# A two-part transformer block: a dense mixture of eight experts becomes a routed one of 40 sorted tiles

## The reference, cut

```python
x = L0_attn_x                                   # (2, 1024, 128): 2 rows, 2048 tokens
xn = _layernorm(x)
x = x + transformer(xn) + moe(xn)

def transformer(x):                             # L = 4 layers, H = 16 heads of 8, F = 512
    for i in range(4):
        x = x + mha(layer_norm(x, ln1), causal + alibi mask)
        xn = layer_norm(x, ln2)
        x = x + gelu(xn @ ffn1.T + b) @ ffn2.T + b
    return layer_norm(x, final)

def moe(xf):                                    # E = 8 experts, the best 2 of a token
    logits = xf @ router_w + router_b
    top_w, sel = top_k(logits, 2)
    gates = softmax(top_w)
    for i in range(8):
        out_i = gelu(xf @ w1[i] + b1[i]) @ w2[i] + b2[i]
        acc = acc + out_i * sum(gates * (sel == i))
    return acc
```

## Time and profile before

| | us |
|---|---|
| time, median of 3 runs | 1606.52 |
| lowest and highest of them | 1605.92, 1608.01 |
| the profiled execution | 1611.84 |
| its span | 1610.0 |
| TensorE busy | 1391.6 |
| VectorE busy | 1046.6 |
| ScalarE busy | 999.9 |
| GpSimd busy | 220.1 |

### The profile page before, as it was taken

The page is one execution under the profiler, slowest core; times in us unless marked ns, Lnnn a source line. Parts: engine busy times, 40 slices in busy tenths (PEclk is TensorE's granted clock), DMA queues, the critical chain, the costliest instruction groups (busy, mean ns, idle before and its releaser), DMA issues.

```text
span 1610.0 us, 36678 instructions
## 1 busy us (share of the span) xinstructions
PE 1391.6 (86%) x12960; PEld 710.0 (44%) x12960; DVE 1046.6 (65%) x2259; ACT 999.9 (62%) x1214; POOL 220.1 (14%) x399
## 2 busy tenths in 40 slices
PE   3789898899889998798988998799998989889974
PEld 2444344454435344353443544344444535444343
DVE  5657666776676765666677766567667766676625
ACT  2055776568666775557865686565866577656841
POOL 4001200121010300112001210013001120011001
PEclk9579999999999999899999999899999999999997
DMA  5111313103021311203120130301211031201010
GB/s 184 56 29 32 97 32 99 30 30 105 24 74 32 96 32 46 75 26 97 32 74 30 30 110 20 99 17 60 82 46 58 19 97 31 78 30 31 5 47 13
DMA packets 82666, 88.87 MB, mean 55 GB/s; under 512 B 8744, under 2 KB 76080, under 8 KB 82480
## 3 DMA queue, kind: packets, MB, share of 16 engines
q1 hardware_dynamic: 82480, 86.43, 17.7%
HBM read 54.15 MB, written 33.55 MB: 54 GB/s over the span
## 4 chain that ended last, share of the span: by engine, by line
PE 67%; DVE 14%; issue 7%; ACT 7%; DMA 2%; SPq 2%; DVEq 0%; POOL 0%; ACTq 0%
PE PS L775 16%; PE PS L740 13%; PE PS L700 12%; PE PS L691 10%; DVE mx L996 7%; PE PS L757 4%; PE PS L721 2%; PE PS L745 2%; ACT PR L586 2%; PE PS L763 2%; DMA x<-orec 1%; DVE hb L920 1%; ACT hb L568 1%; PE PS L725 1%; DVE st L889 1%
## 5 line engine op out<-in xcount | busy, mean ns | idle before, releaser
L996 DVE TENSOR_REDUCE mx<-PS 128x1 f32<-128x512 f32 (+3 forms) x1280 | 773.1, 633 | 354.9 <-PE PS L745 204.1
L586 ACT ACTIVATE PR<-PS 128x1024 f32<-128x1024 f32 (+3 forms) x768 | 610.7, 808 | 441.0 <-PE PS L763 248.1
L740 PE MATMUL PS<-Kop,Qop 64*128 64x512 bf16 (+3 forms) x1536 | 415.5, 341 | 105.0 <-DVE mx L996 93.1
L757 PE MATMUL PS<-Qop,Kop 64*128 64x512 bf16 (+3 forms) x1536 | 368.3, 335 | 19.3 <-ACT PR L586 17.7
L740 PEld LDWEIGHTS PS<-Kop,Qop 64*128 64x128 bf16 x1536 | 128.4, 94 | 557.7 <-DVE mx L996 419.0
L775 PE MATMUL PS<-PR,vbuf 128*32 128x512 f32 (+3 forms) x3072 | 335.0, 509 | 0.4 <-ACT PR L586 0.4
L700 PE MATMUL PS<-wE,hb 128*128 128x128 f32 x1536 | 204.9, 284 | 14.6 <-ACT mrow L558 4.7
L700 PEld LDWEIGHTS PS<-wE,hb 128*128 128x128 f32 x1536 | 182.1, 193 | 33.6 <-issue 14.4
L745 PE MATMUL PS<-idb,mk 64*128 64x64 bf16 x2048 | 196.0, 193 | 0.0
L745 PEld LDWEIGHTS PS<-idb,mk 64*128 64x128 bf16 x2048 | 166.7, 97 | 40.7 <-issue 5.9
L763 PE MATMUL PS<-idb,mk 64*128 64x64 bf16 x2048 | 180.4, 191 | 0.0
(11 more groups left out here) (76 smaller groups left out, 940.6 us busy)
## 6 DMA issues: line engine op xcount, KB each, us to landing
Qop<-qst SPq DMA_DIRECT2D x64, 256.0 KB, 2.9
Kop<-kst SPq DMA_DIRECT2D x64, 256.0 KB, 3.2
...
wE<-in_moe SPq DMA_DIRECT2D x8, 514.0 KB, 3.6
...
Qop<-mrow SPq DMA_DIRECT2D x256, 3.0 KB
```

Of the source, the lines that this page charges most:

```text
L586: act.activation(PR[:, c % 4, :, 0:n], PS[:, 2 * (c % 2):2 * (c % 2) + 2, 0:n], ACT.Exp)\
L740: last = pe.matmul(PS[:, 5 + k % 2, n * e:n * e + n], Qop[r, par, a, P * i:P * i + P], Kop[r, kb, a, 512 * c:512 * c + n], start=True, sto ...
L757: last = pe.matmul(PS[:, 2 * (c % 2) + j, 0:n], Kop[r, kb, a, P * kt:P * kt + P], Qop[r, par, a, q0:q0 + n], start=True, stop=not DIAG[t])
L996: dve.tensor_reduce(mx[:, par, i, 2 * heads[0] + j:2 * heads[-1] + j + 1:2, c], PS[:, 5 + k % 2, 0:n * len(heads)].rearrange("p (h n) -> p ...
```

## The change

The experts are computed for the tokens that chose them alone. In the prologue each of the 4096 pairs of a token and one of its two experts gets a slot: pairs are ranked within their expert by two products with a triangle and with ones, and by scans on VectorE (`routing`, four steps between the maxima of the first unit). Each expert's pairs fill whole tiles of 128; 40 tiles are enough for every distribution. GpSimd writes the normalised tokens to their slots in memory (`scatter`, 32 indirect DMAs in units 0 and 1 of phase 0), to `xs`, which a DMA has filled with zeros. Four tiles are a group, and there are ten groups. For a group SyncE reads the four experts' numbers into a register, loads four weight tiles `wG`, biases `bG` and tokens `xG` (`group_in`); TensorE transposes the tokens ("xt"), makes h and y tile by tile; SyncE writes y to `ys` (`group_out`). In phase 7 GpSimd reads each pair back (`gather`, 32 indirect DMAs in units 0 and 1) and adds both of a token, times their gates, to the input (`combine`, unit 2).

`CHUNKS` now has X0, X1 and two groups, E0 in unit 2 and E1 in unit 3. Phase 0 has one group (E1), odd phases two, even phases one (E1), phase 7 none. X0 and X1 have their GELUs in one slot, (1, 3). X's h goes out through ScalarE, E's through VectorE.

```diff
-CHUNKS = (("E", 0), ("X", 0), ("X", 1), ("E", 1), ("E", 2), ("E", 3))
-HBUF = (0, 1, 0, 1, 0, 1)
-GELUS = ((0, 10), (0, 22), (1, 7), (2, 10), (2, 17), (3, 10))
...
-ON_SCALAR = [(k, f) for k in (0, 3, 5) for f in range(FT)] + [(4, 2), (4, 3)]
+CHUNKS = (("X", 0), ("X", 1), ("E", 0), ("E", 1))
+HBUF = (0, 1, 0, 1)
+GELUS = ((1, 3), (1, 3), (2, 11), (3, 11))
+XT_AT = {2: (2, 3), 3: (3, 3)}
+H_AT = (((0, 18), (0, 19), (0, 20), (0, 21)), ((0, 23), (1, 0), (1, 1), (1, 3)),
+        ((2, 4), (2, 6), (2, 8), (2, 10)), ((3, 4), (3, 6), (3, 8), (3, 10)))
+Y_AT = (((1, 8), (1, 8), (1, 9), (1, 9)), ((1, 11), (1, 12), (1, 13), (1, 14)),
+        ((2, 14), (2, 15), (2, 16), (2, 17)), ((3, 14), (3, 15), (3, 16), (3, 17)))
...
+FIRST_PLAN, LAST_PLAN = plan((3,), False, True), plan((0, 1), True, False, turns=3)
+ODD_PLAN, EVEN_PLAN = plan((0, 1, 2, 3), True, True), plan((0, 1, 3), True, True)
...
+            def group_in(g):
+
+                for i in range(GROUP):
+                    e = sp.value_load(expert_of[0:1, ds(GROUP * g + i, 1)], min_val=0, max_val=E - 1)
+                    sp.dma_start(wG[:, i, :], moe[ds(e, 1), :, :].rearrange("l p n -> (l p) n")).then_inc(S["c_g"], 16)
+                    sp.dma_start(bG[:, i, :], rb_b2[ds(e + 1, 1), :].to_broadcast([P, D])).then_inc(S["c_g"], 16)
+                sp.dma_start(xG[:, :, :], xsv[ds(g, 1), :, :, :].rearrange("g p t d -> (g p) t d")).then_inc(S["c_g"], 16)
...
+            sp.wait_ge(S["c_const"], 16 * 13)
+            sp.dma_start(xs.rearrange("(t p) d -> p t d", p=P), zero[:, :].unsqueeze(1).to_broadcast([P, TILES, D]))\
+                .then_inc(S["c_zero"], 16)
             for b in range(B):
                 for dst, src in ((kfill, kcov), (qfill, qcov)):
...
+                            if half == 0 and j == 2 and f is not None and b == 1:
+                                group_out(group_of(2, b, f), base + number(contents, "y", 2) + 1)
+                                group_in(group_of(3, b, f))
+                            if half == 0 and j == 3:
+                                group_out(group_of(3, b, f), base + number(contents, "y", 3) + 1)
...
+            def scatter(first, last):
+
+                for k in range(first, last):
+                    pool.indirect_dma_start(out=xs[:, :], out_offset=bass.IndirectOffsetOnAxis(ap=slot[:, k:k + 1], axis=0),
+                                            in_=xe[:, k % NT, :], in_offset=None).then_inc(S["c_xs"], 16)
...
+                    if q is None and j < 2:
+                        gather(16 * j, 16 * j + 16)
+                    if q is None and j == 2:
+                        wait_apart(pool, S["c_both"], 16 * RANKS)
+                        for half in range(4):
+                            combine(half // 2, half % 2)
...
-                pe.matmul(PS[:, bank, :], w[:, P * f:P * f + P], src, start=True, stop=True).then_inc(S["s_full"], 1)
...
+                    for m in range(FT):
+                        last = pe.matmul(PS[:, bank, P * m:P * m + P], wG[:, f, P * m:P * m + P], xGT[:, P * f:P * f + P],
+                                         start=True, stop=True)
...
-                    for j in range(4):
-                        t = 4 * c + j
-                        last = dve.scalar_tensor_tensor(out=acc[:, t, :], in0=PS[:, bank, P * j:P * j + P],
-                                                        scalar=gate[:, t, ds(p, 1)], in1=acc[:, t, :],
-                                                        op0=ALU.mult, op1=ALU.add)
+                    last = dve.tensor_tensor(yG[:, :, :], PS[:, bank, :].rearrange("p (t d) -> p t d", t=4), bG[:, :, :], ALU.add)
```

More of the change, by code:

```diff
@@ L33 @@
 U32 = mybir.dt.uint32
+I32 = mybir.dt.int32
 ALU = mybir.AluOpType
@@ L172, in build @@
         rb = sb("rb", [P, E])
-        b2e = sb("b2e", [E, D])
+        tri = sb("tri", [P, P])
+        ones = sb("ones", [P, 2 * P])
+        zero = sb("zero", [P, P])
+        bound = sb("bound", [P, RANKS])
+        place = sb("place", [P, TILES])
         finw = sb("finw", [P, 2, D])
@@ L240, in build @@
         S = {n: sem(n) for n in names}
-        c_wE = [sem(f"c_wE{i}") for i in range(2)]
         c_ldl = [sem(f"c_ldl{i}") for i in range(2)]
@@ L476, in max_parts, with gather, combine @@
                                    ALU.subtract).then_inc(S["s_mpool"], 1)
+            def scatter(first, last):
+                for k in range(first, last):
+                    pool.indirect_dma_start(out=xs[:, :], out_offset=bass.IndirectOffsetOnAxis(ap=slot[:, k:k + 1], axis=0),
+                                            in_=xe[:, k % NT, :], in_offset=None).then_inc(S["c_xs"], 16)
+            def gather(first, last):
+                for k in range(first, last):
+                    pool.indirect_dma_start(out=both[:, k // NT, k % NT, :], out_offset=None, in_=ys[:, :],
+                                            in_offset=bass.IndirectOffsetOnAxis(ap=slot[:, k:k + 1], axis=0))\
+                        .then_inc(S["c_both"], 16)
+            def combine(row, c):
+                tiles = half_tiles(row, c)
+                n = 4 * (2 * row + c)
+                for k, g in enumerate((g1, g2)):
+                    pool.tensor_tensor(both[:, k, tiles, :], both[:, k, tiles, :],
+                                       g[:, tiles].unsqueeze(2).to_broadcast([P, 4, D]), ALU.mult).then_inc(S["s_both"], 1)
+                for k in range(2):
+                    wait_apart(pool, S["s_both"], n + 2 + k)
+                    pool.tensor_tensor(xin[:, tiles, :], xin[:, tiles, :], both[:, k, tiles, :], ALU.add)\
+                        .then_inc(S["s_both"], 1)
             def phase(p, b, f, q, base, contents):
@@ L610, in phase @@
                                     turn_out(base + n, U + 1, 1 - par, 0)
-                                if kind == "h" and which in ON_SCALAR:
+                                if kind == "xt":
+                                    xt_out(base + n)
+                                if kind == "h" and CHUNKS[which[0]][0] == "X":
                                     h_out(base + n, which[0], which[1], b)
@@ L782, in phase @@
                 row = 1 - b
-                place = f if b == 1 else q
-                g0 = 0 if f is None else gelus_before(p)
-                done = [k for k in range(6) if CHUNKS[k][0] == "E" or f is not None]
+                g0 = gelus_before(b, f)
+                done = chunks_of(b, f, q)
                 for j in range(PH):
@@ L957, in v_out, with out_of_bank @@
                                   ALU.add).then_inc(S["s_taken"], 1)
-            def out_of_bank(n, kind, which, p, biases, b, row, bank=7):
+            def out_of_bank(n, kind, which, g, biases, b, row, bank=7):
                 if kind == "h":
@@ L963, in out_of_bank @@
                 if kind == "y":
-                    y_out(n, which, p, biases, row, bank)
+                    y_out(n, which, g, biases, row, bank)
                 if kind == "wo":
@@ L1004, in maximum, with ln_step @@
                         .then_inc(S["s_negm"], 1)
-            def ln_step(idx, row, c, first, now, ready):
+            def ln_step(idx, row, c, first, now, ready, src=xr):
                 (j, k), (j0, s0) = now, first
@@ L1031, in phase @@
                             for n, (spots, kind, which) in enumerate(contents):
-                                if spots[-1] == now and not (kind == "h" and which in ON_SCALAR):
-                                    out_of_bank(base + n, kind, which, p, 4 * p, b, row)
+                                if spots[-1] == now and not (kind == "h" and CHUNKS[which[0]][0] == "X"):
+                                    out_of_bank(base + n, kind, which, group_of(which, b, f) if kind == "y" else 0,
+                                                4 * p, b, row)
                         for c in range(2):
```

360 lines of the change are left out of this document (226 added, 134 removed).

## The result

| | before | after |
|---|---|---|
| time, median (4 runs each), us | 1607.26 | 1631.39 |
| lowest and highest | 1605.92, 1612.86 | 1629.35, 1632.43 |
| span of the profiled execution | 1610.0 | 1630.5 |
| TensorE busy | 1391.6 | 1289.3 |

The ratio is 1.0135 (95% interval 1.0114 to 1.0156): the changed kernel is slower by 24 us, where the forecast was 40 us faster. The page of after, to be read beside the earlier trace rows: engine totals, the granted clock in 40 slices, the chain that ended last.

The account below looks back on a forecast made before the run. TensorE, one fixed order in which waits are lost, was taken as the bound. Prologue, phase and end terms, including GpSimd stalls, summed to -40 us: 1606.5 - 39.7 = 1567 us; own range 1545 to 1592, wider range 1515 to 1615.

Parts of the forecast that it names:

- Unit 0: Phases 1 to 7: h saved before attention's normalise becomes waiting; an h piece, half a y, part of a GELU give -3.5 us.
- Unit 1: Phases 1 to 7: half a y and one h piece go, -2.8 us; with two uncovered GELUs, net +2.1.
- The pair: Two GELUs at slot 3 of unit 1: ScalarE away 6.4 us, TensorE runs ahead 1.5 and idles 4.9.
- An expert's GELU: GELU at slot 11 of expert units, y only from slot 14, nothing behind it: +3.0 us.
- rival D: Slow clock after each of seventeen uncovered GELUs costs 2.7 us, 46 in all: 1613 us; chance 0.12.
- Unit 3 of odd phases: Expert group's unit: less work, but a covered GELU becomes uncovered, so +0.8 us against 42.4 before.
- rival C: Second group's weights come late in odd phases, 6 to 9 us each: 1585 to 1594 us; chance 0.13.
- they overlap: 13 us, no wait: Odd phases' second group: 7 us of issues and reads, 11.5 of loading at 227 GB/s, within 14 us available.
- The bare unit: A unit of 24 slots without FFN fillers: 33.7 us, so unit 2 of even phases changes by -7.9.
- GpSimd's queue: Scatters and gathers at 1.1 us each stall phase 0 unit 2 and phase 7 units 0 and 1: +17.9 us.
- Rival B: GpSimd's scatters and gathers make it slower than before if each exceeds 1.9 us; 1634 us at 2.5; chance 0.13.
- ScalarE's price: Table load 1.28 us without the skill page's further 1.38 us drain per switch, which would give about 1614 us.

Follow-up runs that it names:

- nosw_after: The changed kernel with Identity in place of Gelu, so no table switch: 1554.3 us; the same edit on the kernel before gave 1595.3.
- warm: The changed kernel with unread TensorE products added in unit 0, at slot (1, 5) and in slot 12 of expert units: 1591.7 us.

## Why the prediction was wrong

- **The step that failed most is what taking work out of units 0 and 1 gives.** The runs without switches split the miss. For the GELUs the forecast had booked 10 x 3.0 + 7 x 4.9 for bare blocks, less 3.0 in phase 0 and 7 x 1.3 in unit 0: +52. The runs show 77 - 15 = 62, so 10 us of the miss are there. For all else it had booked -92, and the runs without switches show -41: 50 us are there. In their profiles unit 0 of phases 1 to 6 is 0.8 us longer than before and unit 1 3.4, where -13 and -17 were booked.
- **Unit 0, -3.5 forecast, +0.9 measured.** "What is saved before it becomes more waiting" held: over phases 1 to 6 slots 4 to 9 lose 9.5 us with the h, and slot 10, where TensorE waits for the normalised rows, grows by 10.2. What failed is the -3.5 booked behind that: slots 13 to 23 give 0.6 a phase. The half y gives 0.9 (slot 23, 4.17 to 3.25 us); the h piece of 1.1 stood in slot 10, in the wait itself; for the GELU nothing comes back, slots 21 and 22 take 4.80 us before and 4.73 after. Slots 11 and 12 cost 4.9 us more in six phases at the low clock, and slots 7 to 9 fall to it in phases 3 and 4.
- **Unit 1, +2.1 forecast, +5.0 measured.** The saving of -2.8 failed: at full clock and without switches (nosw_after, four of the six phases, the row below is of phase 1) the unit takes 51.96 us against 52.43 before, -0.5. X1's four h pieces went from slots 4 to 7 to unit 0's end and to slots 0, 1 and 3 and cost their length there, so slots 0 to 4 take 1.7 us more, and slots 5 to 8 give only 2.2. The pair was booked at 4.9, and costs 5.6: its wait is shorter, 3.65, but slots 6 to 8 stand at the low clock. In phase 2 slots 5 to 8 take 9.45 us before, 12.65 after and 10.13 in warm.

```profile
292.57:344.53 51.96, 46.31 (x434) 25.05 (x434) 34.09 (x76) 30.46 (x38) 8.38 (x13) 1.00 0.08 22
```

- **A bare wait was priced as a wait alone.** An expert's GELU was booked at 3.0 us. The wait is 1.41; with what follows, TensorE's own products at the low clock (2.08 against 1.16 us), slots 13 to 16 take 4.2 us more than without switches, on the mean of ten groups. That is rival D's mechanism, and it holds in the rows. `warm` gives back 33 us without the loop's jump, where D had 46. The evidence weighed against it, slots 1 to 14 of phase 0 bare at full clock, was true of a stretch without a wait, and says nothing of the slots behind one. The same rows had 0.67 and 0.77 where a wait or little work stood, and those were the nearer ones.
- **Unit 3 of odd phases, +0.8 forecast, +8.1 measured: rival C.** The step "they overlap: 13 us, no wait" took 227 GB/s from a stretch in which the queue was full. The weights' issues come 1.8 to 2.7 us apart. From 387.63, when the buffers were free, to 403.42, when the tokens behind the weights had landed, it is 15.8 us; and the slots on the way, of which I had counted 14 us, took 12.1 (to 399.72, where the wait of 3.70 begins). The wait of 6 that C was priced by doesn't follow from its own numbers: 18 us less the 14 counted is 4, and the row shows 3.70. C's 18 to 27 us are near what was measured (16.7 in slots 3 and 4, 21.9 for the whole unit) because the low clock behind the wait, which it didn't have, makes up for that.
- **Unit 3 of even phases, +0.8 forecast, +3.1:** some 3 us in phases 2 and 4 are the second gap at the loop's jump, a term that the sum didn't have.
- **The bare unit** was estimated at 33.7 us and is 30.5: even phases' unit 2 gave 11.1 instead of 7.9. The slots of rows 4 at 15 to 23 ran at 0.77, so the estimate had the low clock in it, unnoticed. That the unit with a group came near its forecast (unit 2 of odd phases, +1.0 for +1.6) is luck: the bare unit is 3.2 less, and the fillers cost more, 39.31 - 30.48 = 8.8 us without switches for 9.3 us of work, 0.95 of themselves and not 0.7, with 2.3 to 3.9 for the GELU.
- **GpSimd's queue was right.** d is 1.26 us where I took 1.1; the stalls of 8.5, 1.4 and 8.0 came as 10.9, 2.1 and 6.6, 19.6 us for 17.9. That phase 0 came out at the forecast, -9.2, is luck, as said under the table. Rival B's turning point of 1.9 was not reached.
- **ScalarE's price was right.** The block of the pair is 1.28 + 3.71 + 1.28 with 0.01 and 0.02 us between them. The further 1.38 us of the Trainium skill, "ScalarE: Activation LUTs", section "What ACT_TABLE_LOAD costs", shows in no row of after either. The 1614 that the page's price gave is nearer to the time than the forecast was, but not for its reason.
- **TensorE busy** fell by 102 us, less than the 187 of work that went: y of an expert takes 344 ns an instruction on the mean in after (59.7 us in 320) where it took 284 in 1536. That is 17 of the 85 us; the rest was not split.

What stays open: why dummies in unit 0 and at the pair give nothing alone and 20 us with the third place, when the low clock follows a wait and when it doesn't, and what makes the second gap at the loop's jump.
